# Weight squares handed over in order of use, already transposed, in a graph and mixture-of-experts kernel

## The reference

```
x = x + gnn(layernorm(x)); x = x + ffn(layernorm(x))      # four times, x is 128 x 512

L0 ffn  8 experts: gelu(x @ W1 + b1) @ W2 + b2             W1 512x1024,  W2 1024x512
L1 gnn  relu(h @ W1.T + b1) @ W2.T + b2                    W1, W2 512x512, both transposed
L2 gnn  4 experts, 2 layers: relu(agg @ Wl + bl + h @ Wr)  Wl, Wr 512x512
L2 ffn  8 experts: gelu(x @ w1 + b1) @ w2 + b2             w1 512x2048,  w2 2048x512
L3 gnn  attention over the edges: Wq, Wk, Wv, Wo 512x512, a small FFN of width 32, two norms
L3 ffn  8 experts: silu(x @ w1.T) @ w2.T                   w1 1024x512,  w2 512x1024, transposed
        shared:    (silu(x @ sg_gate.T) * (x @ sg_up.T)) @ sg_down.T            transposed
```

## Time and profile before

| | us |
|---|---|
| runs of the kernel | 626.76 (626.02 to 628.20) |
| the profiled execution | 625.04 |
| its span, first to last instruction | 623.3 |
| L0 FFN, from its first full step to its last product | 53 to 136 |
| L1 graph block and small L1 FFN | 136 to 169 |
| L2 graph block | 169 to 222 |
| L2 FFN | 227 to 428 |
| L3 graph block | 428 to 472 |
| L3 FFN | 472 to 620 |

### The profile page before, as it was taken

The page is one execution under the profiler, slowest core; times in us unless marked ns, Lnnn a source line. Parts: engine busy times, 40 slices in busy tenths (PEclk is TensorE's granted clock), DMA queues, the critical chain, the costliest instruction groups (busy, mean ns, idle before and its releaser), DMA issues.

```text
span 623.3 us, 9254 instructions
## 1 busy us (share of the span) xinstructions
PE 589.2 (95%) x3046; PEld 482.8 (77%) x3046; DVE 500.8 (80%) x592; ACT 430.3 (69%) x529; POOL 105.9 (17%) x112
## 2 busy tenths in 40 slices
PE   4899999998899999999999999999979989999997
PEld 4677888876688876888888888887768778888886
DVE  6799989884689967898888989898776777777773
ACT  4787787844298859677878787876435766666673
POOL 3100000001000000000000000000011656666666
PEclk9999999999999999999999999999999989999999
DMA  7789999983659966989999999996289989999920
GB/s 252 252 299 307 387 386 385 337 300 107 201 185 343 323 231 235 350 329 341 328 342 355 328 357 331 338 324 221 83 188 215 261 213 266 262 262 262 231 54 17
DMA packets 102224, 168.11 MB, mean 270 GB/s; under 512 B 10683, under 2 KB 30140, under 8 KB 102182
## 3 DMA queue, kind: packets, MB, share of 16 engines
q1 hardware_dynamic: 99876, 165.72, 83.1%
q10 hardware_dynamic: 2322, 2.07, 1.2%
HBM read 167.51 MB, written 0.26 MB: 269 GB/s over the span
## 4 chain that ended last, share of the span: by engine, by line
PE 80%; DVE 11%; ACT 5%; issue 2%; POOL 1%; DMA 1%; SPq 0%; ACTq 0%; DVEq 0%
PE pre L839 31%; PE y L839 31%; PE wt L819 6%; PE tp L851 5%; DVE w_lo L1234 3%; PE pre L846 1%; ACT w_hi L551 1%; DVE w_lo L1221 1%; DVE st L1172 1%; DMA ends<-in_edge_weight 1%; PE y L936 1%; POOL rstd L476 1%; ACT w_hi L538 1%; PE wt L1063 1%; PE pre L952 0%
## 5 line engine op out<-in xcount | busy, mean ns | idle before, releaser
L1234 DVE TENSOR_TENSOR w_lo<-raw,w_hi 128x2048 fp32r<-128x2048 f32 x115 | 259.0, 2287 | 40.0 <-ACT w_hi L551 39.5
L551 ACT ACTIVATE w_hi<-raw 128x2048 fp32r<-128x2048 f32 x116 | 218.6, 1918 | 0.0
L839 PE MATMUL pre<-w_hi,x_hi 128*128 128x512 f32 x292 | 85.1, 404 | 4.0 <-ACT x_hi L556 3.3
L538 ACT ACTIVATE w_hi<-wt 128x512 fp32r<-128x512 f32 x88 | 52.2, 600 | 51.5 <-PE wt L819 50.9
L839 PE MATMUL pre<-w_lo,x_hi 128*128 128x512 f32 x292 | 83.3, 398 | 1.4 <-DVE w_lo L1234 0.9
L606 ACT ACTIVATE hT_hi<-tp 128x512 fp32r<-128x512 f32 x66 | 39.6, 600 | 65.1 <-PE tp L851 65.1
L1221 DVE TENSOR_TENSOR w_lo<-wt,w_hi 128x512 fp32r<-128x512 f32 x88 | 58.5, 668 | 31.2 <-ACT w_hi L538 31.0
L839 PE MATMUL pre<-w_hi,x_lo 128*128 128x512 f32 x292 | 82.9, 397 | 0.0
L839 PE MATMUL y<-w_hi,hT_hi 128*128 128x512 f32 x280 | 81.9, 414 | 0.0
L475 POOL TENSOR_SCALAR rstd<-mv 128x1 f32<-128x1 f32 x11 | 3.0, 272 | 441.1 <-DVE mv L1173 441.1
L839 PE MATMUL y<-w_lo,hT_hi 128*128 128x512 f32 x280 | 75.9, 392 | 0.4 <-DVE w_lo L1234 0.4
(11 more groups left out here) (266 smaller groups left out, 689.6 us busy)
## 6 DMA issues: line engine op xcount, KB each, us to landing
raw<-in_L_ffn_w SPq DMA_DIRECT2D x80, 1024.0 KB, 7.0
raw<-in_L_ffn_W SPq DMA_DIRECT2D x32, 1024.0 KB, 10.2
raw<-in_L_ffn_w SPq DMA_DIRECT2D x32, 512.0 KB, 11.2
raw<-in_L_gnn_Wr SPq DMA_DIRECT2D x8, 1024.0 KB, 6.2
raw<-in_L_gnn_Wl SPq DMA_DIRECT2D x8, 1024.0 KB, 6.6
raw<-in_L_gnn_W SPq DMA_DIRECT2D x2, 1024.0 KB, 7.1
raw<-in_L_ffn_sg_gate SPq DMA_DIRECT2D x2, 1024.0 KB, 8.1
raw<-in_L_ffn_sg_up SPq DMA_DIRECT2D x2, 1024.0 KB, 7.7
```

Of the source, the lines that this page charges most:

```text
L538: act.activation(w_hi[:, g % SPLIT_SLOTS, q], wt[q % 2][:], ACT.Copy).then_inc(w_hi_ready, 1)
L551: act.activation(w_hi[:, g % SPLIT_SLOTS], raw[:, g % RAW_SLOTS], ACT.Copy).then_inc(w_hi_ready, 4)
L839: last = pe.matmul(dst, xs[:, k], ws[:, k], start=start and i == 0, stop=stop and i == len(passes) - 1 and bias is None)
L1234: dve.tensor_tensor(w_lo[:, i], raw[:, g % RAW_SLOTS], w_hi[:, i].bitcast(F32), ALU.subtract).then_inc(w_lo_ready, 4)
```

## The change

The host function `kernel()` passes the weights in another order in memory. All 156 squares stand in one array `chunks` in order of use, and those that the reference uses transposed are transposed there. The small weights are also laid out as they lie on the chip. In the kernel every chunk takes the same path (load, round, split, product) in one loop of loads, and both ways of turning weights are gone, with their semaphores, GpSimd's subtraction and the permuted order of h. In the L3 FFN the router moves from step 2 to step 0, and the fourth chunk is rounded and split ahead of the pipeline. In the L3 graph block the turning quarters between its steps become `keep_clock` calls; in the L1 graph block nothing takes their place. The bytes loaded stay the same.

```diff
-BRIDGE = {"l0g": 0, "l0f": 4, "l1f": 37, "l2g": 23, "l2f": 30, "l3g": 28, "l3f": 14}
+BRIDGE = {"l0g": 0, "l0f": 4, "l1f": 37, "l2g": 23, "l2f": 30, "l3g": 28, "l3f": 44}
...
             # SyncE
-            def load_up(g, rows, it=None):
-            def load_down(v, columns, it=None):
...
-                sp.dma_start(raw[:, g % RAW_SLOTS], source).then_inc(landed[g % RAW_SLOTS], 16)
+                sp.dma_start(raw[:, g % RAW_SLOTS], A["chunks"][at(g, RAW_SLOTS, it)].rearrange(
+                    "(c p) n -> p c n", p=P)).then_inc(landed[g % RAW_SLOTS], 16)
+            for g in range(2 * RAW_SLOTS):
+                load(g)
+            with sp.Fori(0, CHUNKS // RAW_SLOTS - 2) as it:
+                for g in range(2 * RAW_SLOTS, 3 * RAW_SLOTS):
+                    load(g, it)
+            for g in range(CHUNKS // RAW_SLOTS * RAW_SLOTS, CHUNKS):
+                load(g)
...
-                    small(rw_n[0:7, :], A["L2_ffn_rw"], "rw_in")
-                    small(rw_n[7:15, :], A["L3_ffn_gate_w"], "rw_in")
+                    small(rwT[:, 0, :, 0:7], A["L2_ffn_rw"], "routers_in")
+                    small(rwT[:, 1], A["L3_ffn_gate_w"], "routers_in")
...
             # GpSimd
-            split_block(BLOCKED[0])
-            ...
             # ScalarE
-            small(side[:, :, 0:P], emb[0], "emb_in")
-            small(side[:, :, P:2 * P], emb[1], "emb_in")
+            small(side[:], A["L0_gnn_emb"], "emb_in")
...
-                if turned(g):
-                    for q in range(4):
-                        round_turned_quarter(g, q, it)
-                else:
+                act.wait_ge(landed[g % RAW_SLOTS], at(arrived(g), 16, it))
+                act.activation(w_hi[:, g % SPLIT_SLOTS], raw[:, g % RAW_SLOTS], ACT.Copy).then_inc(w_hi_ready, 4)
+            def round_half(g, first):
+                ...
+                act.activation(w_hi[:, g % SPLIT_SLOTS, part], raw[:, g % RAW_SLOTS, part], ACT.Copy)...
...
+                    if pipe.lead and s == 0:
+                        after0()
+                    if s < pipe.n:
+                        if not (pipe.lead and s == 0):
+                            round_chunk(g + AHEAD, it)
+                        g += 1
+                    if pipe.lead and s == 1:
+                        round_chunk(g + AHEAD)
...
             # TensorE, product(): 16 transposes of the chunk two ahead
-                    if i % 3 == 0 and turned_within(g) is not None:
-                        turn_weights(turned_within(g), i // 3, it)
...
-                    pe.transpose(ms[:, 0:P], ident[:], ident[:])
+                    pe.transpose(wt[1][:, 0:P], ident[:], ident[:])
...
             # TensorE, L1 graph block
-            for q in range(4):
-                turn_weights(G_L1G + 1, q)
...
             # TensorE, L3 graph block
-            turn_weights(G_L3F, 0)
-            turn_weights(G_L3F, 1)
+            keep_clock(6)
...
-            turn_weights(G_L3F, 2)
-            turn_weights(G_L3F, 3)
+            keep_clock(6)
...
-            turn_weights(G_L3F + 1, 0)
+            keep_clock(3)
...
-            turn_weights(G_L3F + 1, 1)
-            turn_weights(G_L3F + 1, 2)
-            keep_clock(24)
+            keep_clock(32)
...
-            turn_weights(G_L3F + 1, 3)
+            keep_clock(4)
...
-            turn_weights(G_L3F + 2, 0)
-            turn_weights(G_L3F + 2, 1)
-            turn_weights(G_L3F + 2, 2)
-            turn_weights(G_L3F + 2, 3)
...
             # VectorE
-            def transpose_block(g, q, it=None):
-            def split_turned_quarter(g, q, it=None):
+            def split_part(g, first, n):
+                wait_rounded(dve, g, first + n)
+                part = slice(first, first + n)
+                dve.tensor_tensor(w_lo[:, g % SPLIT_SLOTS, part], raw[:, g % RAW_SLOTS, part], ...)
...
+                    if pipe.lead and s == 0:
+                        router()
...
             # VectorE, L1 graph block
-            statistics("l1g", X[:])
-            split_turned_quarter(G_L1G + 1, 0)
-            split_turned_quarter(G_L1G + 1, 1)
-            normalise_x("l1g")
-            split_turned_quarter(G_L1G + 1, 2)
-            split_turned_quarter(G_L1G + 1, 3)
+            layer_norm("l1g")
+            split_chunk(G_L1G + 1)
...
             # host
+def _laid_out(inputs):
+    ...
+    order += [w["L1_gnn_W1"].T, w["L1_gnn_W2"].T]
+    ...
+    gate, up = _squares(w["L3_ffn_sg_gate"].T), _squares(w["L3_ffn_sg_up"].T)
+    order += _in_order([gate[0], up[0], gate[1], up[1]] + [m for e in w["L3_ffn_w1"] for m in _squares(e.T)],
+                       [m for e in [w["L3_ffn_sg_down"]] + list(w["L3_ffn_w2"]) for m in _squares(e.T)], L3F.lead)
+    chunks = np.stack(order)
```

More of the change, by code:

```diff
@@ L86 @@
 BL_COL = 2048
[L89 to L132, removed]
-def arrived(g):
[L137 to L141, removed]
+def arrived(g):
+    return 16 * (g // RAW_SLOTS + 1)
 NORMED = ["l0g", "l0f", "l1g", "l1g_out", "l1f", "l2g", "l2f", "l3g", "l3g_mid", "l3g_out", "l3f"]
@@ L392, in square @@
-            def square(w):
-                return w.rearrange("(c p) n -> p c n", p=P)
-            def steps(pipe, w1, w2):
-                def step(s, it=None):
-                    g = pipe.chunk(s)
-                    if s < pipe.n:
-                        load(g, w1(s, it), it)
-                        g += 1
-                    if s >= 2:
-                        load(g, w2(s - 2, it), it)
-                peeled = 8 if pipe.g0 == 0 else 4
-                for s in range(peeled):
-                    step(s)
-                with sp.Fori(0, pipe.loops() - (peeled - 4) // 4) as it:
-                    for s in range(peeled, peeled + 4):
-                        step(s, it)
-                for s in range(4 + 4 * pipe.loops(), pipe.n + 2):
-                    step(s)
@@ L414, in _ @@
-            steps(L0F, lambda u, it: w1_unit(A["L0_ffn_W1"], 2, u, it),
-                  lambda u, it: w2_unit(A["L0_ffn_W2"], 2, u, it))
-            load(G_L1G, square(A["L1_gnn_W1"]))
-            load(G_L1G + 1, square(A["L1_gnn_W2"]))
-            g = G_L2G
-            for s in range(E4 + 2):
-                for e, layer in ((s, 0), (s - 2, 1)):
-                    if 0 <= e < E4:
-                        load(g, square(A["L2_gnn_Wr"][e, layer]))
-                        load(g + 1, square(A["L2_gnn_Wl"][e, layer]))
-                        g += 2
@@ L898, in step @@
                         g += 1
-                    if s == 0:
+                    if s == 0 and not pipe.lead:
                         router()
@@ L1274, in step @@
                     g = pipe.chunk(s)
-                    if pipe.lead:
-                        turning = G_L3F + 3 if s == 0 else turned_within(g) if s < pipe.n else None
-                        for q in range(4):
-                            if turning is not None:
-                                split_turned_quarter(turning, q, it)
-                            if s < pipe.n:
-                                transpose_block(BLOCKED[s], q, it)
+                    if pipe.lead and s == 0:
+                        router()
                     if s < pipe.n:
-                        split_chunk(g + AHEAD, it)
+                        if not (pipe.lead and s == 0):
+                            split_chunk(g + AHEAD, it)
                         g += 1
-                    if s == pipe.route == 2:
-                        router()
                     if s == 3 and seeded:
@@ L1633 @@
 def kernel(**inputs):
-    import numpy as np
     import concourse.bacc as bacc
```

309 lines of the change are left out of this document (95 added, 214 removed).

## The result

The changed kernel takes 591.7 us (589.4 to 593.7, median of 4 runs) where the kernel before takes 627.5 (626.0 to 629.5, 4 runs beside it): a ratio of 0.943, with an interval of 0.937 to 0.948. The gain is 35.8 us; the forecast was 38.2. The profiled execution took 593.6 us with a span of 591.9, 31.4 less than the 623.3 before, and its mean granted clock was 0.986. The two runs at 0.994 took 589.4 and 589.8 us, the two at 0.986 took 593.64 and 593.65: one program, and its time went with its clock.

The account below looks back on a forecast made before the run. TensorE was taken as the bound, with weight transposes on the L3 FFN's path. Gains 34.9 + 1.6 + 1.3 + 0.4 = 38.2 us take the median 626.76 to 588.6 us; own range 586.5 to 591, wider range 583.5 to 596.

Parts of the forecast that it names:

- Part 1: L3 FFN: without weight turns TensorE's step falls from 7.71 to 5.92 us, 148.3 to 113.4, gaining 34.9 us.
- The reserve of VectorE: L3 FFN: VectorE ends at 91% of TensorE's step, with 0.5 us to spare.
- Part 3: L3 graph block: turning groups become keep_clock transposes, fewer waits between engines; 1.3 us gained, bounds 0.1 to 2.
- Supply and layout: Weight loads: 354 GB/s needed in the L3 FFN, supply at no cost; contiguous squares don't reach the path.
- rival A: L3 FFN: supply or VectorE bounds just above TensorE, step 6.15 to 6.4 us, kernel 592 to 596; chance 0.15.
- the bounds of 6.2 to 7.0: Landing of contiguous squares: 0.8 us sooner than 7.0 us, or no change.
- Part 2: L1 graph block: removed turns bring the first product sooner, less a slow clock; 1.6 us gained, between 1.3 and 3.0.
- Part 4: The rest: 0.4 us gained in L0 FFN's step 1; edge lists 0; L2 graph block and L2 FFN unchanged.
- 3.4 / 2 = 1.7 at most, less what falls beside ScalarE's rounding, so 1.4: L1 graph block: price of 3.4 us at half clock after TensorE idles about 2.2 us, taken as 1.4 us.
- the "2.2" of my last paragraph: L0 FFN: expected to be shorter by 2.2 us, among the signs to look for in the changed kernel's chain.
- rival B: Clock falls in more places, at the L3 FFN's start and between L3 graph block steps: 591 to 592 us; chance 0.08.
- the likeliest case: Whole kernel: the forecast itself, 588.6 us from the median, own range 586.5 to 591; chance 0.60.

Follow-up runs that it names:

- b_turns_back: Changed kernel with 16 unused identity transposes put back on TensorE in each of 15 of the L3 FFN's 18 steps; 619.0 us, ratio 0.985.
- a_fill_l1: Changed kernel with 18 unread transposes in TensorE's idle time before the L1 graph block's first turn; 588.9 us.
- a_all_three: Changed kernel with L1 idle-time fill, quarter splits moved behind the normalisation, and 62 instead of 44 bridge transposes into the L3 FFN; 586.6 us, ratio 0.936.
- b_ups_alone: Kernel before with only L3's up and gate squares (and shared ones) turned by the host, down squares going the old way; 623.8 us, ratio 0.9935.

## Why the prediction was right, and where it was off

**Part 1, the L3 FFN** (34.9 forecast, 33.0 found) was right in mechanism and size. The difference of two steps of the kernel before, 1.79 us, is the price of the turns, shown by their return in `b_turns_back`. The step became 5.92 us, TensorE the whole of it. The reserve of VectorE that I put at 0.5 us measures 0.6. Of the 1.9 us missing, 1.6 are the first product at half clock (4.61 instead of 3.02), which belongs to Part 3's seam.

**Supply and layout.** 354 GB/s were forecast as needed, and 355 came; rival A did not. But the DMA engines read as full there (1.03), so there was little to spare. Contiguous squares brought nothing to the path. Their landing of 7.4 us lies outside the bounds of 6.2 to 7.0, and these bounds rested on a wrong reading: I had taken all squares of the 7.0 us group for strided, and more than half were not the earlier trace rows. Stage by stage the landing came later in the L2 FFN (7.3 us against 6.9) and sooner in the L0 FFN (7.4 against 9.8, 60 to 110 us).

**Part 2, the L1 graph block,** with Part 4's 0.4 (together 2.0 gained forecast, 1.85 lost). This is the step that failed: "3.4 / 2 = 1.7 at most, less what falls beside ScalarE's rounding, so 1.4". The block's first product does come sooner, at 140.83 against 142.72: 1.9 us of the 3.4 that I had without the clock. It stands 5.58 us after the L0 FFN's last product, where I had put 5.1 without a slow clock; with the fill it is 5.17. That the clock would fall after an idle time of some 2.2 us was right (it was 2.36). But it stayed at half for 6.8 us, not 3.4, and fell again at 159.8, and from the block's first product to that of the L2 graph block this cost 3.7 us (30.42 against 26.68) instead of 1.4. The removed turns had been a load on the path and had at the same time kept TensorE busy; `a_fill_l1` gives 2.7 us back with 18 idle transposes. The second fall costs 1.4 us of the 3.7 (28.11 against 26.68 in `a_fill_l1`) and has another cause, which stays open: it comes with the fill too.

**Part 3, the L3 graph block** (1.3 forecast, 0.2 found). From the start of the L2 FFN's last sum to the L3 FFN's first product it is 43.41 us against 43.63. The softmax came 0.4 sooner, as worked out, but the add behind the small FFN only 0.8 in all (34.82 us after the start against 35.62), not 0.4 and 0.8: the small FFN itself gave 0.5. Then two things went wrong. GpSimd's 1/sqrt(var) took 0.8 us longer beside splits that now read two SBUF operands, and with that only 0.2 was left; I had written that the splits are "of the same length as before", which is true of VectorE and says nothing of its neighbour. And TensorE's idle time was 2.41 us, not some 1.8, so the fall that I had taken as a "no" came; its price of 1.6 stands in Part 1. `a_all_three` removes both.

**Part 4.** The L2 FFN's step is 6.15 us as before. The L0 FFN started 0.7 us later: the edge lists' DMA landed 1.5 us sooner, the bound I had drawn, but only 0.8 of that was left at 18 us, a fall of the clock at 19.8 us then cost 1.7, and the 0.4 of the small transposes can't be told apart from this. That fall is in two of the nine traces that share this start, so it belongs to the execution and not to the change alone. The turning groups went as forecast (1.8 us of 1.76). The L0 FFN thus ended 1.15 us sooner and not by the "2.2" of my last paragraph, which had added the 0.4.

**The sum,** from the two chains, after against before: the L0 FFN ends 1.15 us sooner, the L2 graph block starts 1.85 later, the L3 FFN starts 1.63 later, and its last product ends 31.4 sooner. So everything ahead of the L3 FFN, where I had expected 3.3 us gained, lost 1.6, and the L3 FFN gave 33.0. What came is rival B, a clock that falls in more places. One of them I had named (the start of the L3 FFN), two not (19.8 and 159.8 us), and the fall that I did expect was twice as long. B was priced at 591 to 592 us; the measured 591.7 lies there, 0.7 above the likeliest case's own range. That it is one and not the other is partly luck: two of the four runs took 589.4 and 589.8 us at a clock of 0.994, inside the likeliest case's range, and by that clock an estimated 7 us of them were at half speed, the others at 0.986 about 17.

## What to carry to other kernels

The price of work on a full engine is the difference of two steady steps of the same trace; it can be read before anything is built, and it held to 0.01 us here. Before removing filler-like work from TensorE, ask at each seam what else fills the idle time: here the clock fell after 2.4 us of waiting in seven traces of seven, and filling it gave 2.7 us back in one block. Then look at the whole stretch again: a second fall, 14 us after the first, had looked like a part of the first and did not go with it. Two halves of a change need not add up: when two routes share the buffers and queues of one step, remove both or measure both, since one alone gave 4 us here, and both 36. And when an edit gains nothing in all, read its single steps: half of GpSimd's work gone showed as four steps of 5.92 us, and the loads took them back.

## What the runs showed of the hardware that was not expected

A 1 MB load of a 512x512 square landed in 5.3 us in the median (156 loads) from rows 319 KB apart and in 7.4 us when the square lay contiguous, in the same kernel, read into rows of 2 KB in both. The Trainium skill ("DMA: Bandwidth & Descriptors", Latency and other measured facts) reports slower copies at row pitches of large powers of two and advises to pad or to lay tiles out contiguously; 319 KB is no such pitch, and here contiguous was the slower of the two.

Loads of 32 partitions took 14.3 us to land with 1 KB runs and with 16 KB runs alike, and with them the DMA engines read as full at 255 to 261 GB/s, where whole squares went at 355. After an idle time of 2.36 or 2.37 us on TensorE the clock fell to half in seven traces of seven, for 3.4, 6.8 or 10.2 us; with the idle time filled this fall did not come. Another, 14 to 17 us after the first had ended, came with the fill and without it, with no idle time over 0.7 us ahead of it in the filled kernel; and in one kernel the clock fell after an idle time of 1.03 us. GpSimd's one-element instructions lost 0.4 us each beside a VectorE split with two SBUF operands; its 128x512 subtractions in `b_ups_alone` took 1.29 us in the median and up to 3.35.
